# Selective scan: sums over the states by accumulating transposes, and the drives of 7 of a group's 32 steps made by GpSimd, their decays written to PSUM

## The reference

```python
def _rmsnorm(h, w):
    var = jnp.mean(h.astype(jnp.float32) ** 2, axis=-1, keepdims=True)
    return (w * (h * lax.rsqrt(var + EPS))).astype(h.dtype)

def _mamba(x, ...):                      # D_MODEL 256, D_INNER 512, D_STATE 16, D_CONV 4, DT_RANK 16
    xz = jnp.einsum('bld,ed->ble', x, in_proj_w)
    u, z = jnp.split(xz, 2, axis=-1)
    # causal convolution of 4 taps over the tokens, per channel
    u = jax.nn.silu(conv(u) + conv_b)
    dbc = jnp.einsum('bld,ed->ble', u, x_proj_w)
    dt, Bm, Cm = jnp.split(dbc, [DT_RANK, DT_RANK + D_STATE], axis=-1)
    dt = jax.nn.softplus(jnp.einsum('blr,dr->bld', dt, dt_proj_w) + dt_proj_b)
    A = -jnp.exp(A_log)

    def step(s, inp):
        d, u_i, b_i, c_i = inp
        s = s * jnp.exp(d[..., None] * A) + (d * u_i)[..., None] * b_i[:, None, :]
        y = jnp.einsum('bdn,bn->bd', s, c_i)
        return (s, y)
    _, ys = lax.scan(step, s0, inputs)
    y = jnp.moveaxis(ys, 0, 1) + u * D_skip
    y = y * jax.nn.silu(z)
    return jnp.einsum('ble,de->bld', y, out_proj_w)

x0 = _rmsnorm(x, rms1_w)
x = _mamba(x0, ...) + x
x = x + _mlp(_rmsnorm(x, rms2_w), ...)   # three layers of 512, relu
```

## Time and profile before

| | us |
|---|---|
| median of 3 runs | 2705.36 (2701.47 to 2721.03) |
| the profiled execution | 2706.49 |
| its span | 2704.4 |
| mean granted TensorE clock | 0.943 of full |

### The profile page before, as it was taken

How to read it: one execution, slowest core, us unless ns; L and a number is a source line. 1 busy time by engine, 2 the same in 40 slices (tenths; PEclk the granted TensorE clock), 3 DMA queues, 4 the chain that set the end, 5 groups by cost and what they waited for, 6 DMA issues and landing times. The chain is left out here.

```text
span 2704.4 us, 45426 instructions
## 1 busy us (share of the span) xinstructions
PE 2399.8 (89%) x15293; PEld 1439.5 (53%) x15293; DVE 1984.3 (73%) x4362; ACT 1491.8 (55%) x3321; POOL 1310.7 (48%) x1257
## 2 busy tenths in 40 slices
PE   4678989898989898979999988988986999999697
PEld 1224444444444444547777755655663666566555
DVE  4999999999999999626766746777775454556545
ACT  5666777777777776433333323554563666655522
POOL 1777777777777777424332322444464232221401
PEclk7889999999999999989999987998997999999899
DMA  5443433343433344211000034323303000000100
GB/s 162 124 130 122 133 120 128 120 129 121 132 119 129 122 127 131 74 35 40 1 1 1 1 75 72 70 51 64 72 12 104 16 17 21 17 18 17 48 14 9
DMA packets 134312, 196.03 MB, mean 72 GB/s; under 512 B 23953, under 2 KB 58898, under 8 KB 134082
## 3 DMA queue, kind: packets, MB, share of 16 engines
q1 hardware_dynamic: 132098, 190.24, 24.5%
q0 software_dynamic: 960, 2.62, 0.3%
q10 hardware_dynamic: 1024, 0.26, 0.1%
HBM read 153.95 MB, written 13.63 MB: 62 GB/s over the span
## 5 line engine op out<-in xcount | busy, mean ns | idle before, releaser
L398 POOL TENSOR_TENSOR ma_seen<-ma_state,ma_cs 128x1024 f32<-128x1024 f32 x256 | 603.2, 2360 | 325.3 <-DVE ma_state L951 309.2
L951 DVE TENSOR_TENSOR_SCAN ma_state<-ma_decay,ma_last,ma_drive 128x512 f32<-128x512 f32 x512 | 650.3, 1270 | 0.0
L587 PE MATMUL ma_acc<-ma_seen,ident 128*128 128x512 f32 x1024 | 492.1, 611 | 46.8 <-POOL ma_seen L398 46.7
L938 DVE TENSOR_TENSOR ma_drive<-ma_weight,ma_bs 128x512 f32<-128x512 f32 x512 | 356.6, 697 | 40.2 <-ACT ma_weight L793 11.8
L587 PEld LDWEIGHTS ma_acc<-ma_seen,ident 128*128 128x128 f32 x1024 | 195.5, 196 | 300.5 <-issue 208.7
L803 ACT ACTIVATE ma_decay<-ma_dt,ma_a_neg 128x512 f32<-128x512 f32 x512 | 338.0, 709 | 0.0
L2076 DVE CUSTOM_DVE_ANT_0 sw_score<-sw_score,both_band 128x256 f32<-128x256 f32 (+1 forms) x512 | 197.4, 447 | 52.7 <-PE sw_score L1890 40.9
L2014 ACT ACTIVATE sw_prob<-sw_turned 128x512 f32<-128x512 f32 (+1 forms) x256 | 135.5, 581 | 180.3 <-PE sw_turned L1904 156.0
L104 POOL TENSOR_TENSOR moe_h_low<-both_V,light_wqkv 128x512 fp32r<-128x512 f32 x80 | 105.1, 1314 | 244.1 <-DVE light_wqkv L100 236.6
L1812 POOL TENSOR_SCALAR_AFFINE_SELECT sw_prob<-sw_prob 128x512 f32<-128x512 f32 x128 | 84.4, 659 | 214.1 <-ACT sw_prob L2014 214.1
L1536 DVE TENSOR_TENSOR both_V<-both_V,moe_up 128x512 f32<-128x512 f32 x80 | 55.0, 687 | 117.4 <-PE moe_up L1325 76.2
(11 more groups left out here) (547 smaller groups left out, 5453.7 us busy)
## 6 DMA issues: line engine op xcount, KB each, us to landing
ma_bs<-bc_rows SPq DMA_DIRECT2D x256, 256.0 KB, 3.2
ma_cs<-bc_rows SPq DMA_DIRECT2D x256, 256.0 KB, 3.2
both_wide<-both_kh SPq DMA_DIRECT2D x28, 192.0 KB, 4.3
both_wide<-both_qh SPq DMA_DIRECT2D x20, 256.0 KB, 4.5
x_rows<-X SPq DMA_DIRECT2D x1, 4096.0 KB
light_rows<-li_y SPq DMA_DIRECT2D x32, 128.0 KB, 1.7
out_dram<-li_o SPq DMA_DIRECT2D x32, 128.0 KB, 1.8
X<-in_L_attn_x_dram SPq DMA_DIRECT2D x1, 3584.0 KB, 14.3
```

The source lines that it names most:

```text
L398: g.tensor_tensor(out=seen[n % RR][:, :, :], in0=state[n % SR][:, :, :], in1=each(cs[n % CR][:, :], 2), op=ALU.mult).then_inc(S["seen_full ...
L587: ins = t.matmul(accs(mm), K["ident"][:, :], seen[n % RR][:, mm, :], start=False, stop=(n % NS == NS - 1))
L938: v.tensor_tensor(out=drive[mm][:, :], in0=weight[mm][:, :], in1=bs[n % CR][:, :], op=ALU.mult).then_inc(S["drive_done"], 1)
L951: v.tensor_tensor_scan(state[n % SR][:, mm, :], decay[s % DR][:, :], drive[mm][:, :], last[:, k, m:m + 1], ALU.mult, ALU.add).then_inc(S[" ...
```

## The change

The change has four parts. POOLED names the seven steps of a group that are made another way.

1. In a pooled step GpSimd makes the drive of both parts in one operation, into `pdrive` in SBUF (`pool_drives`), called behind `weigh` three steps earlier. VectorE makes none. The two PSUM banks of `drive` are free then, and ScalarE writes the decays into them (`bank_decay`): the one for part 0 as the last thing of its body for the step before, behind the scan of part 0 of the step before; the one for part 1 as the first thing of the step's own body.
2. `sums` becomes 8 transposes of 128x128 that accumulate in PSUM, so that tokens lie on the partitions of `acc`. `starts`, `gates` and the gate follow this layout: `starts` is now 8 matmuls of 128 columns per half instead of 2 of 512.
3. The out projection wants channels on partitions, so TensorE turns the gated values back (`back`, 16 transposes a group, in steps 3 to 5) and ScalarE copies them (`turned_back`, four of 128x512, in steps 4 to 6). `mix` moves two steps later.
4. The ring `seen` goes from 4 to 3 buffers. On GpSimd `dt_weight` of the second half moves from step 6 to 12 and the second root with the residual add from 8 to 10. On ScalarE the scaling `scaled2` moves from step 10 to 12, the squares from 7 to 9.

```diff
-DR, SR, RR, CR = 6, 4, 4, 3
+DR, SR, RR, CR = 6, 4, 3, 3
+POOLED = (3, 6, 9, 12, 19, 22, 26)
...
-    if q in (3, 4, 5, 6) and one:
-        found.append(("mix", i - 1, q - 3))
+    if q in (3, 4, 5) and one:
+        found += [("back", i - 1, j) for j in ((0,), (1, 2), (3,))[q - 3]]
+    if q in (5, 6, 7, 8) and one:
+        found.append(("mix", i - 1, q - 5))
...
+            def pool_drives(n):
+
+                if n >= Q * GROUPS or not on_pool(n):
+                    return
+                i, q = divmod(n, Q)
+                pool.wait_ge(b_in[n % CR], 16 * (n // CR + 1))
+                pool.wait_ge(S["wdt_done"], 2 * i + q // NS + 1)
+                since(pool, "scan_done", 2 * max((k + 1 for k in range(n) if on_pool(k)), default=0))
+                g.tensor_tensor(out=pdrive[:, :, :], in0=wdt[:, :, :], in1=each(bs[n % CR][:, :], 2), op=ALU.mult).then_inc(S["pool_drive_done"], 1)
...
                     weigh(i, q)
+                    pool_drives(Q * i + q + 3)
...
-                    if q == 6:
+                    if q == 12:
                         dt_weight(i, 1)
-                    if q == 8 and one:
+                    if q == 10 and one:
                         root("2", ss2, rstd2, i - 1)
                         adds(i - 1)
...
             def sums(n):
                 pe.wait_ge(S["seen_full"], n + 1)
-                for mm in range(2):
-                    ins = t.matmul(accs(mm), K["ident"][:, :], seen[n % RR][:, mm, :], start=False, stop=(n % NS == NS - 1))
+                last_ = n % NS == NS - 1
+                for j in range(GT):
+                    for mm in range(2):
+                        ins = t.matmul(accs(j, mm), seen[n % RR][:, mm, j * P:(j + 1) * P], K["ident"][:, :], is_transpose=True,
+                                       start=False, stop=(last_ and j % 2 == 1 and mm == 1))
                 ins.then_inc(S["seen_used"], 1)
...
+            def bank_decay(n, mm):
+
+                i, q = divmod(n, Q)
+                h, k = divmod(q, NS)
+                m = 2 * h + mm
+                since(act, "scan_done", 2 * n - 1 + mm)
+                a.activation(drive[mm][:, :], dt[:, m, :], ACT.Exp, scale=a_neg[:, m, k:k + 1]).then_inc(S["bank_decay_done"], 1)
...
                 for q in range(Q):
                     n = Q * i + q
+                    if on_pool(n):
+                        bank_decay(n, 1)
                     if n:
                         keeps(n - 1)
...
-                    if q == 10 and one:
+                    if q == 12 and one:
                         scaled2(i - 1)
...
+                    if on_pool(n + 1):
+                        bank_decay(n + 1, 0)
...
                 if mm == 0:
                     since(dve, "seen_full", n - SR + 1)
                     since(dve, "kept", n - SR + 1)
...
+                if on_pool(n):
+                    if mm == 0:
+                        dve.wait_ge(S["pool_drive_done"], pooled_before(n) + 1)
+                    dve.wait_ge(S["bank_decay_done"], 2 * pooled_before(n) + mm + 1)
+                    keep, add = drive[mm][:, :], pdrive[:, mm, :]
```

111 lines of the change are left out of this document (77 added, 34 removed).

## The result

| | before | changed kernel |
|---|---|---|
| median, us | 2708.39 (2701.47 to 2721.03, 4 runs) | 2761.82 (2761.28 to 2764.96, 4 runs) |
| ratio | 1 | 1.0204, interval 1.0172 to 1.0235 |
| span of the profiled execution, us | 2704.4 | 2759.6 |
| mean granted TensorE clock | 0.943 | 0.902 |
| start of the last gate (end of the scan phase), us | 1130.5 | 1186.1 |

The forecast was 2714 with a range up to 2750; the time is above both. The whole loss lies in the scan phase: its last gate starts 55.6 us later, and the span is 55.2 us longer. A row on the gate gives this; its last number is the start of the last one. The layers behind it took 1566 to 1592 us in the profiled executions (2740.5 - 1174.1 in e8, 2744.1 - 1152.0 in e17), so a difference of a few us in the whole time says less than one in the end of the phase.

What follows compares the result with a forecast made beforehand. VectorE's queue was taken to bound the scan phase. Groups 1 to 6 +25, group 0 -1, group 7 -8, weight copies -11, end +3 gave +8 us: 2714 forecast, range 2672 to 2750.

Steps and rivals of the forecast that it cites:

- 1.5 us per pooled step: VectorE, each pooled step: two drives off and two shorter scan gaps save 1.5 us, 84 us in all without waits.
- Steps 2 to 13, GpSimd bound, 43.4 us: Step 2's second scan to first convolution tap: GpSimd's queue and ScalarE behind it take 43.4 us, 2.4 longer than before.
- A root costs 477.57 - 473.85 - 2.33 = 1.39: GpSimd's queue in steps 2 to 13: each of two small root computations adds 1.39 us to its work.
- about 1.6 us of wait: Step 3: ScalarE reaches the decay late, about 1.6 us, costing nothing of its own because GpSimd's queue is longer.
- Steps 18 to 19, +2.9: Last tap to step 19's scan: ScalarE's table loads and Silus precede the decay; 2.4 us become 5.4, +2.9.
- Steps 19 to 26, 27.1 us: ScalarE's queue up to the decay of 26 makes the stretch 27.1 us, gaining 0.6 where 3.0 was on offer.
- Weight copies, -11: End of each group: VectorE's 11.0 us of waits for ScalarE's weight copies counted as gone.
- The end, +3: After the last group: two copies and their transposes for turning back stand in the open, some 3 us.
- The start of a sum: TensorE, start of an accumulation: 16 instructions of 128 columns, between 1.8 and 6.9 us, taken as 3.4.
- forecast 25 - 11 = 14: Groups 1 to 6 lose 4.1 us each, 25 in all; the vanished weight-copy waits give back 11.
- The second rival: Lower TensorE clock delays units ahead of decays of 6, 9, 12, 26 and step 3's sums: 31 us, 2745; chance 0.26.
- The test sentence: Prediction wrong if VectorE's waits for ScalarE stay below 50 us in sum, or a group takes less than 131 us.

Runs made afterwards that it cites:

- e8: Changed kernel with sums, starts, gates and out projection as before the change, so the seven pooled steps' drives alone; 2751.9 us, 1.0150 to before.
- e17: Kernel of e7 with each idle matmul replaced by eight accumulating transposes of zeros in the same five steps; 2732.5 us, 1.0096 to before.
- e10: Changed kernel with only steps 15, 22, 27 pooled and ScalarE's second-norm scaling moved behind the second projection at step 13; 2682.9 us, 0.9897 to before.
- e7: Kernel of e1 with an idle matmul adding zeros behind the sums of steps 27 to 30 and 0; 2730.5 us, 1.0092 to before.
- e1: Changed kernel with GpSimd's root of the next group's first norm moved ahead of the products of steps 3 and 6; 2740.5 us, 1.0121 to before.
- e15: Kernel of e7 with the idle matmul also behind the sums of steps 11 to 14, 16 and 17; 2725.5 us, 1.0075 to before.
- e4: Changed kernel with an idle matmul adding zeros behind the sums of each step but the last of a half; 2788.0 us, 1.0294 to before.
- e16: Kernel of e10 with an idle matmul adding zeros behind the sums of steps 11 to 14, 16 and 17; 2682.3 us, 0.9921 to before.

## Why the prediction was wrong

Point by point, by the terms of its sum, for the group shown above.

- *1.5 us per pooled step.* Right: 1.6 in the group of e10 without a wait.
- *Steps 2 to 13, GpSimd bound, 43.4 us.* This is the step that failed. From 486.47 + 1.27 to the first tap at 537.03 it is 49.3 us. GpSimd's queue itself was counted right, as e7 shows with 40.0 and 43.4 us, but it was counted to run without a gap; it was idle 3.98 us at step 3. Two sentences failed. "A root costs 477.57 - 473.85 - 2.33 = 1.39" counted the root as work of GpSimd, and did not ask who waits for its result: ScalarE's `scaled1`, now behind 2.36 us more of GpSimd's work, ahead of the bank decay of 6 (e1: 23 us in all). And of the "about 1.6 us of wait" at step 3 it said "so it costs nothing of its own": the wait is 5.39, since I took ScalarE's queue there from its own instructions and left out that they wait for TensorE's two units, 2.3 and 2.5 us, half of it by the clock (e7). Late at 3, GpSimd's products and the root are later still, so the two add up: 5.9 us in this group, 3.3 by the root (49.3 to 46.0, e1) and 2.6 by the clock (46.0 to 43.4, e7).
- *Steps 18 to 19, +2.9.* Right: from the last tap's end, 563.31 + 0.74 (its row in the timeline), to 569.51 it is 5.5 us, forecast 5.4.
- *Steps 19 to 26, 27.1 us.* It is 598.89 - 569.51 = 29.4. The piece of 12.6 from the first unit of the step size on is right to 0.1 (585.54 to 598.08). The piece ahead was mis-sized: it holds two waits for TensorE, 0.79 and 1.54, where I had put 0.5.
- *Weight copies, -11.* Right. *The end, +3:* not to be seen; behind the last gate come 1573.5 us, before 1573.9, and these layers scatter by more.
- *TensorE.* Eight accumulating transposes take 1.04 us at full clock, as the rows of before said. The start of a sum takes 1.95 for its 16 instructions; I had taken 3.4.

Summed over the phase, by the gates of step 2: up to the one in group 1, 200.16 against 197.16, +3.0 (forecast -1); from there to that of group 7, 1069.14 against 1008.86, another +57.3 (forecast 25 - 11 = 14); behind it -4.8 (forecast -8, though the half of 10.5 that it names is 5). Most of what was missed, 43 of 51 us, lies in the six groups with everything beside them. The root and the clock are 23.2 + 11.4 = 34.6 us by the last gates of e1 and e7; the stretch from 19 to 26 is 2.3 in the group shown and less in the others, whose wait at 26 is 1.9 to 3.4 us instead of 4.52.

The second rival, slower by the clock, had the nearest number (2745), and that by luck. The first half of its condition came: 0.84 between 460 and 590 us. The clock was shown to cost VectorE time at the units ahead of step 3, some 11 us of the 55, a place that the rival did not name; of the four that it named, 6 went with the root, 26 did not move with the clock (e15), and at 9 and 12 no run took the clock apart from the added work. The Trainium skill, TensorE: Matmul & The Clock Gate, section "What's actually happening", says that the throttled level is the default and activity releases it; the traces agree (0.96 before, 0.84 in the changed kernel, 0.95 with the fill of e4), but the fill also shows that a full clock, bought by work ahead of the units, cost 26 us.

The test sentence, wrong "if a group takes less than 131 us", looked to the wrong side. The tests that told were the others: no gap on GpSimd (there are two), the tap 43 to 44 us after step 2 (49), some 80 us of waits (over 134) and a group of 135 to 140 us (146). What stays open is how much of the wait at 3 beyond the clock is ScalarE's exponential and squares, and how much GpSimd's late products ahead of TensorE's sums; no run took them apart.

## What to carry to other kernels

When an operation that was made ahead of time becomes one that can't be early, list for each place everything that stands before it in its engine's in-order queue, and follow each entry to what it waits for on the other engines, small results too; then place it where that list is empty. Such waits do not go away singly: taking one out brings the waiting engine earlier to the next, or down to the engine that is full (here GpSimd, 43.4 us for the stretch). Three well placed steps (e10, 1.0% faster) did what seven could not, and the filled clock is worth having only at the few places where a late unit is waited for.

## What the runs showed of the hardware

- Matmuls and transposes that only add zeros raised TensorE's granted clock: from 0.84 to 0.95 between 460 and 590 us in e4 (matmuls), from 0.88 in e1 to 1.00 between 440 and 484 us in e7 (matmuls) and e17 (transposes).
- The same two matmuls of a unit took 2.07 us near the lower level (0.56 between 476 and 485 us in the changed kernel) and 1.12 at the higher (1.00 in e7); the same eight took 4.78 us at a mean of 0.69 (e10, 534 to 539 us) and 3.63 at 1.00 (e16, the same stretch).
- ScalarE wrote a decay to a PSUM bank about as fast as to SBUF: a pair takes 1.29 us (492.32 has one), a pair to SBUF 1.32 (the one that starts at 560.09).
